# Image loads and stores in eight pieces of four rows, one per tile step

## What is computed

```python
shortcut = x                                   # [B, H, W, C]
x = layer_norm(x, gamma1, beta1)
x = jnp.roll(x, shift=(-4, -4), axis=(1, 2))
x = window_attention(x, w_qkv, b_qkv, w_proj, b_proj)
x = jnp.roll(x, shift=(4, 4), axis=(1, 2))
x = shortcut + x
shortcut = x
x = layer_norm(x, gamma2, beta2)
x = gelu(x @ w_fc1 + b_fc1) @ w_fc2 + b_fc2
x = shortcut + x
```

## Time and profile before

| | us |
|---|---|
| median of 3 runs | 4975.95 (4972.98 to 4988.05) |
| profiled execution, its own time | 4969.82 |
| its span, first to last instruction | 4967.9 |
| TensorE matmuls busy | 4324.0 |
| VectorE busy | 3374.5 |
| GpSimd busy | 3008.3 |
| ScalarE busy | 2772.6 |

### The profile page before, as it was taken

The page is one execution under the profiler, slowest core; times in us unless marked ns, Lnnn a source line. Parts: engine busy times, 40 slices in busy tenths (PEclk is TensorE's granted clock), DMA queues, the critical chain, the costliest instruction groups (busy, mean ns, idle before and its releaser), DMA issues.

```text
span 4967.9 us, 174574 instructions
## 1 busy us (share of the span) xinstructions
PE 4324.0 (87%) x66384; PEld 3040.0 (61%) x66384; DVE 3374.5 (68%) x9081; ACT 2772.6 (56%) x5921; POOL 3008.3 (61%) x6254
## 2 busy tenths in 40 slices
PE   4888888988888988888889888888888888898987
PEld 2566665666666666666666666666566666666665
DVE  5666666767666767666666666766676666676765
ACT  1555555655555555555556555555555565555554
POOL 4666655666666666666566666665665665666654
PEclk9999999999999999999999999999999999999999
DMA  4444454445454444454454454444444544544442
GB/s 94 83 83 85 83 87 83 81 87 93 78 88 91 81 86 84 87 84 81 87 93 76 87 89 83 87 82 88 85 83 87 91 78 86 91 81 87 85 82 59
DMA packets 1467388, 420.49 MB, mean 85 GB/s; under 512 B 1450295, under 2 KB 1452731, under 8 KB 1466557
## 3 DMA queue, kind: packets, MB, share of 16 engines
q1 hardware_dynamic: 1466556, 409.32, 45.8%
HBM read 31.56 MB, written 25.17 MB: 11 GB/s over the span
## 4 chain that ended last, share of the span: by engine, by line
PE 46%; DMA 15%; DVE 10%; POOL 10%; issue 8%; SPq 8%; ACT 2%; POOLq 0%; DVEq 0%; ACTq 0%
PE ps_s L557 12%; DMA qkt<-qk 10%; PE bank L569 8%; PE bank L436 7%; PE bank L531 4%; POOL hid L1083 4%; DVE smax L880 3%; PE ps_t L514 3%; DMA xt<-xs 3%; DVE hid L918 3%; SPq L346 3%; PE ps_s L503 2%; POOL xs L1076 2%; PE bank L469 2%; PE ps_s L494 2%
## 5 line engine op out<-in xcount | busy, mean ns | idle before, releaser
L1022 POOL TENSOR_TENSOR rstd<-vare,half 128x2 f32<-128x2 f32 x518 | 360.1, 695 | 1081.2 <-DVE vare L858 1081.2
L918 DVE TENSOR_TENSOR hid<-hid 128x512 f16<-128x512 f32 x768 | 600.8, 782 | 528.5 <-POOL hid L1083 507.4
L557 PE MATMUL ps_s<-ht,w_fc 128*128 128x512 f16 x3840 | 878.7, 381 | 17.3 <-DMA ht<-xs 7.3
L569 PE MATMUL bank<-w_fc,hid 128*128 128x192 f16 x9216 | 851.0, 247 | 7.8 <-DVE hid L918 5.6
L880 DVE TENSOR_REDUCE smax<-ps_s 128x12 bf16<-128x768 f32 x512 | 488.2, 954 | 512.6 <-PE ps_s L494 499.7
L569 PEld LDWEIGHTS bank<-w_fc,hid 128*128 128x128 f16 x9216 | 774.1, 98 | 82.6 <-issue 55.9
L671 ACT ACTIVATE pt<-ps_t 128x768 f16<-128x768 f32 x512 | 415.4, 811 | 677.6 <-PE ps_t L514 674.6
L1083 POOL TENSOR_SCALAR hid<-hid 128x512 f16<-128x512 f32 x768 | 564.0, 734 | 310.6 <-ACT hid L679 309.1
L679 ACT ACTIVATE hid<-ps_s,b_fc 128x512 f32<-128x512 f32 x768 | 530.2, 690 | 342.4 <-PE ps_s L557 167.4
L557 PEld LDWEIGHTS ps_s<-ht,w_fc 128*128 128x128 f16 x3840 | 361.7, 98 | 459.9 <-issue 63.6
L436 PE MATMUL bank<-w_qkv,xt 128*128 128x384 f16 x2560 | 544.3, 346 | 47.6 <-DMA xt<-xs 45.2
(11 more groups left out here) (113 smaller groups left out, 7717.5 us busy)
## 6 DMA issues: line engine op xcount, KB each, us to landing
x_img<-in_x_dram SPq DMA_DIRECT2D x32, 768.0 KB, 5.9
out_dram<-y_img SPq DMA_DIRECT2D x32, 768.0 KB, 5.7
xt<-xs SPq DMA_TRANSPOSE x512
qkt<-qk SPq DMA_TRANSPOSE x512, 3.8
ot<-os SPq DMA_TRANSPOSE x512, 2.4
ht<-xs SPq DMA_TRANSPOSE x512, 2.3
stage<-in_L_conv_fc_w_dram SPq DMA_DIRECT2D x2, 384.0 KB, 4.0
stage<-in_L_conv_w_fc_dram SPq DMA_DIRECT2D x2, 384.0 KB, 4.5
```

The source lines that it names most:

```text
L557: last = mm(ps_s[:, u % 2, :], w_fc1[layer][:, part, m * 128:(m + 1) * 128], ht[:, p % 2, blk, :], start=(i == 0), stop=(i == 4))
L569: mm(bank[:, 0:C], hid16[:, hs, m, tok], w_fc2[layer][:, ws, m, :], start=(m == 0 and i == 0), stop=False)
L918: v.tensor_tensor(hid16[:, 1, m, :], hid[:, u % 2, :], hid16[:, 0, m, :], ALU.subtract)\
```

## The change

The image is moved in eight pieces, `half_slab(view, h)`: four rows of the image, starting at row (4 + 4h) mod 32, so 96 partitions x 2 x 128 elements, 96 KB. `load` and `store` take a piece number h. Each piece has a semaphore of its own for loading and one for storing. In the step loop the piece numbered like the tile is loaded at the step s with s + 9 in layer 0, and stored at the step s with s - 9 (places 0 and 1 of a group) or s - 13 (places 2 and 3) in layer 1; a piece waits for both tiles of its pair (`rank | 1`). GpSimd waits, per tile, for the two pieces that the tile reads; ScalarE waits for the two pieces of a pair of tiles at each even tile.

```diff
+SLABS = SIDE // WS
...
+def half_slab(view, h):
+
+    row = (SHIFT + h * SHIFT) % SIDE
+    return view[:, :, row * SIDE:(row + SHIFT) * SIDE]
...
-        x_loaded = sem("x_loaded")
-        y_stored = sem("y_stored")
+        x_loaded = [sem(f"x_loaded{h}") for h in range(2 * SLABS)]
+        y_stored = [sem(f"y_stored{h}") for h in range(2 * SLABS)]
...
+            def load(image, h):
+
+                sp.dma_start(half_slab(x_img, h), half_slab(x[image].rearrange("(k p) h w -> p k (h w)", k=2), h))\
+                    .then_inc(x_loaded[h], 16)
+
+            def store(image, h):
+                sp.dma_start(half_slab(out[image].rearrange("(k p) h w -> p k (h w)", k=2), h), half_slab(y_img, h))\
+                    .then_inc(y_stored[h], 16)
...
-                        sp.dma_start(x_img[:, :, :], x[0].rearrange("(k p) h w -> p k (h w)", k=2)).then_inc(x_loaded, 16)
+                        for h in range(2 * SLABS):
+                            load(0, h)
...
             when(sp, "x_ordered", TILES - 1)
-            load(1)
+            for h in range(2 * SLABS):
+                load(1, h)
...
-                if live(s + 10) and visit(s + 10)[1:] == (0, TILES - 1) and rank(s + 10) + 1 < IMAGES * TILES and s + 10 >= TILES:
-                    ge("x_ordered", rank(s + 10))
-                    load(rank(s + 10) // TILES + 1)
-                if live(s - 9) and visit(s - 9)[1:] == (1, TILES - 1):
-                    ge("y_ready", rank(s - 9))
-                    store(rank(s - 9) // TILES)
+                if live(s + 9) and s + 9 >= TILES and visit(s + 9)[1] == 0 and visit(s + 9)[0] + 1 < IMAGES:
+                    ge("x_ordered", rank(s + 9) | 1)
+                    load(visit(s + 9)[0] + 1, visit(s + 9)[2])
+                for n, places in ((s - 9, (0, 1)), (s - 13, (2, 3))):
+                    if live(n) and visit(n)[1] == 1 and n % GROUP in places:
+                        ge("y_ready", rank(n) | 1)
+                        store(visit(n)[0], visit(n)[2])
...
-                    if t == 0 and image > 0:
-                        act.wait_ge(y_stored, 16 * image)
+                    if t % 2 == 0 and image > 0:
+                        for h in (t, t + 1):
+                            act.wait_ge(y_stored[h], 16 * image)
...
-            pool.wait_ge(x_loaded, 16)
             for t in range(TILES):
+                for h in (t, t ^ 1):
+                    pool.wait_ge(x_loaded[h], 16)
                 order_tile(0, t)
...
-                    pool.wait_ge(x_loaded, 16 * (image + 1))
+                    for h in (t, t ^ 1):
+                        pool.wait_ge(x_loaded[h], 16 * (image + 1))
```

More of the change, by code:

```diff
@@ L379, in slot @@
                     o_turn(s - 1)
-                if live(s + 10) and visit(s + 10)[1:] == (0, TILES - 1) and rank(s + 10) + 1 < IMAGES * TILES and s + 10 >= TILES:
-                    ge("x_ordered", rank(s + 10))
-                    load(rank(s + 10) // TILES + 1)
-                if live(s - 9) and visit(s - 9)[1:] == (1, TILES - 1):
-                    ge("y_ready", rank(s - 9))
-                    store(rank(s - 9) // TILES)
+                if live(s + 9) and s + 9 >= TILES and visit(s + 9)[1] == 0 and visit(s + 9)[0] + 1 < IMAGES:
[5 more added lines that the diff above has]
+                        store(visit(n)[0], visit(n)[2])
             run(slot)
-            sp.wait_ge(y_stored, 16 * IMAGES)
-            sp.wait_ge(x_loaded, 16 * IMAGES)
+            for h in range(2 * SLABS):
+                sp.wait_ge(y_stored[h], 16 * IMAGES)
+                sp.wait_ge(x_loaded[h], 16 * IMAGES)
         W_DMAS = [9, 4, 5, 1]
```

## The result

The changed kernel takes 4841.97 us (median of 4 runs, 4820.42 to 4850.49) against 4977.37 us: a ratio of 0.9716, 95% interval 0.9694 to 0.9738, so 2.8% or 135 us faster. The forecast was 4797 us. The profiled execution has a span of 4848.1 us, 119.8 us less than before.

What follows compares the result with a forecast made beforehand. The TensorE, 87% busy, was taken as the limit, broken twice per image by a transposition queued behind a big copy. 4969.8 - 255 - 80 + 154 + 2.5 = 4791 us, so 4797 us for the median; range 4690 to 4925 us.

Steps and rivals of the forecast that it cites:

- the gross gain: TensorE time saved by removing the long stalls (255 us) and the slow-clock work behind them (80 us): 335 us.
- The two long stalls: At L485, waits for qkt queued behind each image load or store, 61 events, would go: 255 us saved.
- The slow clock: TensorE work at the lower clock behind the long stalls would go, 1.3 us per event: 80 us saved.
- The issue in every step: SyncE's piece issue puts qkt back 0.62 us in every step, 1.2 us per four-step group: 154 us added.
- The slacks read from the earlier trace: Spare time of qkt before the scores in a group's four steps: 5.3, 0.2, 0.1 and 0.5 us.
- The piece's transfer: Queue time of a piece ahead of qkt, expected to overlap: taken as 0, bounds 0 and 0.5 us per step.
- Waits added: SyncE's waits before each piece, and ScalarE's and GpSimd's waits for single pieces: cost 0.
- Ahead of the loop: SyncE issues eight pieces instead of one, putting back the first fc1 weights: 2.5 us added, between 0 and 3.6.
- (a): Rival: SyncE's added issues hide almost wholly, only 40 us given back, 4683 us; chance 0.13.
- (b): Rival: every issue in a group's three short steps reaches the TensorE in full, 276 us back, 4920 us; chance 0.15.
- (c): Rival: piece delays qkt by transfer and issue; break-even 4976 us, chance 0.04; slower, up to 5386 us, chance 0.08.
- the 250 us: Sign at the scores: L485 and L494 together still holding over 250 us of waits would prove the prediction wrong.

Runs made afterwards that it cites:

- floor run: The changed kernel without any image load or store inside the loop (images 0 and 1 loaded ahead, one image stored at the end): 4686.59 us, ratio 0.9419.
- quarter-bytes run: The changed kernel with each piece at its place and with its 192 descriptors, but moving 24 KB in place of 96: 4824.90 us, ratio 0.9675.
- whole images in the right step: The kernel before, whole-image DMAs still ahead of qkt, load one step later and store two, where qkt has slack: 4694.02 us, 4694.06 us when repeated.
- the best pieces: The changed kernel with each of the eight pieces issued behind the next qkt instead of ahead of it: 4686.42 us, 4684.58 us when repeated.
- the run meant for it: The kernel with whole-image DMAs where qkt has slack (4694 us), plus ten empty SyncE instructions ahead of each qkt: 4692.81 us, ratio 0.944.

## Why the prediction came out as it did

**Direction and mechanism: right.** The long stalls were the transfer ahead of qkt (an eighth of the bytes at the old place removes most of it), and the return is the pieces' place ahead of qkt (one DMA later it is gone). The forecast of 4797 us is 45 us below the measured 4842, and the whole of that lies in the gross gain, 335 us against 290.

**The two long stalls, 255 us: the stalls well priced, the gain too high.** In the trace of before 60 qkt transpositions (I had counted 61) follow an image DMA, and the scores behind them wait 254.9 us, 4.25 us each; the mean of two samples, 5.60 and 3.14, was near to that by luck. But the floor run has only 282.6 - 80.2 = 202 us less at L485, 3.3 us per event, and 193 us with L494. The term that was mis-sized is what is left once the stall is gone. I took off the ordinary waits of the *other* 44 steps, but a step that loses its long stall keeps an ordinary wait of its own, which stood hidden in the long one. The same 60 steps wait 39.2 us in the floor run, 0.65 us each, and the steps right behind them 14.5 us where they had waited 0.3.

**The slow clock, 80 us: a little low.** PE's busy time fell by 105.7 us in the floor run. Gross gain by the medians: 290 us where I had 335. The stalls' term was 62 us too high and the clock's 26 us too low; the waits for the maximum (13.7 us longer) and for xt (5.3 us shorter) make up the rest.

**The issue in every step, 154 us: right in size, in part by luck.** The medians give 4842 - 4687 = 155 us (the two profiled executions 170). The profile has 144 us more at the scores, 17 us less for xt and 5 us less for the maximum, and 58 us more of PE's busy time (4275.9 against 4218.3): the small stalls bring the lower clock back too, for which I had set nothing. The waits alone come to some 122 us. The slacks read from the earlier trace rows were good: 3 x 0.62 - 0.8 = 1.1 us per group, and 144/128 = 1.1 at the scores. That L494's wait, booked as "issue", is one for qkt is borne out: 68.1 us in the floor run, 131.3 with one DMA ahead of qkt, 210.0 with two.

**The piece's transfer, taken as 0:** about 20 us by the quarter-bytes run, within the bounds. The median qkt lands 3.9 us after its issue, against 3.7 in the floor run.

**Waits added, taken as 0:** right. In the loop no engine's list of waits has one for an x_img load or a store. **Ahead of the loop:** VectorE's wait went from 3.84 to 5.99 us, 2.2 us where 2.5 was taken.

**Rivals.** (a) was wrong, the issues don't hide. (b) overstated the first issue, 276 us against 155. The break-even of (c), 1.14 us per piece, was nearly reached when a second issue was added, 0.62 + 0.50 = 1.12 us, by issues and not by a transfer as (c) has it. The kernel was then 1.9% slower than before and not the same: of the 381 us given back (155 + 226) 139 are PE's busy time, for which no rival had a term. The Trainium skill ("DMA: Bandwidth & Descriptors", "Rules for kernel authors") says to coalesce many small transfers. The runs agree in so far as one small DMA more per step made the kernel slower than before, and whole images in the right step come within 0.2% of the best pieces, with 448 DMAs fewer. They differ for the change itself, which was faster with eight pieces. The prediction's 2.0 us plus bytes / 436e3 is given in the Trainium skill ("DMA: Bandwidth & Descriptors", "Anatomy of one DMA — SWDGE (gpsimd) path") for DMAs that GpSimd issues. These are SyncE's, and an image landed in 5.9 us where that sum has 3.8.

**What I said the profile would show.** Pieces landing in about 2 us, an issue of 0.52 us, a qkt issue as long as before (1.43 us in the median) and L506 above 58.9 us came out. L497 below 80 us did not (161.2), nor idle stretches of at most 3 us (L506 has one of 3.2), nor a clock over 0.98 (0.979). L497 and L506 together hold 292.5 us. That is above the 250 us at which I had called the prediction wrong by (b) or (c), and yet neither came. The sign was set too low by the mis-sized term: my own sum was 341.5 - 255 + 154 = 240 us, and the floor alone has 148.3 us where 341.5 - 255 would leave 86.5. SyncE waits for y_img only at the end of the program, 22.1 us in two waits (23.6 us in one before), and in no place for x_win.

**What stays open:** whether the delay of SyncE alone, without a DMA, has the whole price; the run meant for it did not delay anything. The traces only say that the piece puts qkt's issue back by 0.62 us and its landing by 0.2 us more.

## What to carry to other kernels

Before cutting a large transfer up, look for the step in which the transfer that queues behind it has slack: its slack is the end of the work ahead of the waiting instruction, less the landing, both in the timelines. A DMA issued ahead of a latency-critical one puts that one back by its issue time, and what of it no slack covers is lost in every step. So put small transfers behind the critical one on the same queue, and a large one in a step with slack: behind qkt in a short step the whole image only moved the stall to xt. Another queue did not help here. When a long stall is priced, take off the ordinary wait that the same step and the next will have without it, and add the work that runs at the lower clock after it.

## What the runs showed of the hardware

- A copy of 768 KB issued 0.50 us after a transposing DMA, from another engine's queue, held that transposition back: the matmuls that needed it started 9.5 us after its issue (an ordinary one lands in 3.8 us). While the copy ran, the two queues started 150 and 145 packets in 2.5 us, of 4 KB and of 256 bytes. The qkt transpositions next to such a copy landed 8.5 us after their issue in the median; with the copy at least 1.4 us behind them on the same queue it was 4.0 us.
- 96 KB in 192 rows of 512 bytes landed in 2.2 us from HBM and 1.9 us to HBM, 768 KB in 192 rows of 4 KB in 5.9 and 5.7 us; the issue took 0.52 us in both cases.
- An image ahead of it on the same queue held up the issue of a transposition too, and not only its landing: in the kernel before the 60 qkt issues behind an image lasted 2.86 us in the mean, the others 1.49 us. With the pieces the mean is 1.49 us again.
- Short stalls bring the lower clock too. With (1 - clock) x 2 x span, 387 us are spent at it before, 204 us in the changed kernel and 65 us in the floor run. The changed kernel has 281 waits at the scores, none over 3.2 us; the floor run has 173, none over 3.0 us.
